# One attention and mixture-of-experts block: each raw chunk of `w13` fetched in two halves, behind the rounding of the probabilities

## What is computed

```python
mod = (_silu(L0_c) @ L0_wmod).reshape(8, 6, 1, -1)
sa, ca, ga, sb, cb, gb = (mod[:, i] for i in range(6))      # ga, gb kept away from zero
h = _layernorm(x) * (1 + ca) + sa
x = x + ga * infini_attention(h, W_q, W_k, W_v, W_o, beta)  # 16 heads, segments of 64 tokens
h = _layernorm(x) * (1 + cb) + sb
x = x + gb * moe(h, router_w, w13, w2)                      # 8 experts, the best 2 of each token
# infini_attention, per segment, with a memory M and z carried along:
#   A = beta * (s(q) M) / (s(q) z) + (1 - beta) * softmax(causal q k^T) v
#   M += s(k)^T (v - (s(k) M) / (s(k) z));  z += sum s(k)
# moe: logits = h router_w^T; gate, up = split(h w13[e]); y = (silu(gate) * up) w2[e]
```

## Time and profile before

| | us |
|---|---|
| median of 3 executions | 1365.4 |
| the three executions | 1365.4, 1361.44, 1370.28 |
| the profiled execution's own time | 1369.37 |
| its span in the profile | 1367.3 |

### The profile page before, as it was taken

How to read it: one execution, slowest core, us unless ns; L and a number is a source line. 1 busy time by engine, 2 the same in 40 slices (tenths; PEclk the granted TensorE clock), 3 DMA queues, 4 the chain that set the end, 5 groups by cost and what they waited for, 6 DMA issues and landing times. The chain is left out here.

```text
span 1367.3 us, 54718 instructions
## 1 busy us (share of the span) xinstructions
PE 1192.2 (87%) x20142; PEld 1016.3 (74%) x20142; DVE 939.0 (69%) x2509; ACT 706.6 (52%) x1391; POOL 927.2 (68%) x989
## 2 busy tenths in 40 slices
PE   3499999999889998989613899999999999999995
PEld 0277778787767777767413699999999999999994
DVE  2389889998888998878668655555555555555552
ACT  2267878887878887877632222323322232322321
POOL 3158989998988898888910466666666666666643
PEclk8599999999999999999855999999999999999998
DMA  9811333334443434443461454545455455555540
GB/s 225 175 55 51 76 91 94 91 96 109 110 97 88 104 104 99 109 99 97 112 216 16 105 99 91 98 92 98 91 101 101 92 95 95 98 94 98 99 75 1
DMA packets 124476, 134.54 MB, mean 98 GB/s; under 512 B 26090, under 2 KB 103986, under 8 KB 124098
## 3 DMA queue, kind: packets, MB, share of 16 engines
q0 software_dynamic: 32592, 56.77, 22.0%
q1 hardware_dynamic: 89762, 67.46, 20.1%
q10 hardware_dynamic: 1872, 6.82, 1.8%
HBM read 63.60 MB, written 44.04 MB: 79 GB/s over the span
## 5 line engine op out<-in xcount | busy, mean ns | idle before, releaser
L1131 PE MATMUL psum<-xT,xall 128*128 128x256 f16 x3408 | 396.6, 273 | 2.5 <-DVE xT L1118 0.9
L1131 PEld LDWEIGHTS psum<-xT,xall 128*128 x3408 | 331.1, 98 | 40.9 <-issue 3.2
L1191 POOL DMA_INDIRECT out<-yo,sidx x142 | 226.4, 1594 | 198.4 <-DVE yo L1182 172.1
L1139 ACT ACTIVATE sg<-psum 128x512 f32<-128x512 f32 x142 | 84.7, 597 | 317.6 <-PE psum L1131 282.8
L1144 DVE SCALAR_TENSOR_TENSOR hf<-psum,sg 128x512 f32<-128x512 f32 x142 | 98.2, 691 | 209.2 <-ACT sg L1139 205.3
L1101 POOL DMA_INDIRECT grow<-moe_rows,gidx x142 | 142.6, 1004 | 99.5 <-DVE sidx L992 56.5
L1165 PE MATMUL psum<-w2s,hT 128*128 x1704 | 197.7, 273 | 2.6 <-DVE w2s L1217 2.4
L1165 PEld LDWEIGHTS psum<-w2s,hT 128*128 128x128 f16 x1704 | 166.5, 98 | 22.5 <-issue 3.2
L1151 ACT ACTIVATE hT<-hf 128x512 f16<-128x512 f32 x142 | 89.5, 630 | 111.4 <-DVE hf L1144 104.6
L569 POOL TENSOR_TENSOR pT<-sc,pT 128x1024 f16<-128x1024 f32 x64 | 136.5, 2133 | 10.1 <-ACT pT L565 10.1
L1155 DVE TENSOR_TENSOR hT<-hf,hT 128x512 f16<-128x512 f32 x142 | 98.3, 692 | 57.0 <-ACT hT L1151 40.4
(11 more groups left out here) (217 smaller groups left out, 2429.9 us busy)
## 6 DMA issues: line engine op xcount, KB each, us to landing
stk<-qk SPq DMA_DIRECT2D x384, 64.0 KB
moe_rows<-hrows SPq DMA_DIRECT2D x128, 128.0 KB, 2.4
out<-xall SPq DMA_DIRECT2D x128, 64.0 KB, 2.1
xall<-in_x SPq DMA_DIRECT2D x8, 896.0 KB, 18.1
raw<-in_w ACTq DMA_DIRECT2D x13, 512.0 KB, 5.5
raw<-in_w SPq DMA_DIRECT2D x8, 512.0 KB, 7.9
grow<-moe_rows,gidx POOLq DMA_INDIRECT x142
out<-yo,sidx POOLq DMA_INDIRECT x142
```

Source lines behind the costliest of these rows:

```text
L1131: i = k.e.matmul(bank[:, n * LONG:(n + 1) * LONG], w13s[:, bass.ds(ex_reg * (G * 4 * I) + ((2 * c + b_) * 2 * I + col), P)], xT[:, k.b, a, ...
L1139: done(k.e.activation(sg[:, half, :], bGate[half][:, :], ACT.Silu, scale=1.0 / W_SCALE), "sg")
L1191: k.e.indirect_dma_start(out_rows, bass.IndirectOffsetOnAxis(ap=sidx[:, n:n + 1], axis=0), yo[:, k.v, q, :], None, bounds_check=B * T - 1, ...
```

## The change

A chunk is now fetched by two DMAs of 128x512 (256 KB) instead of one of 128x1024. The first half (columns 0 to 511, the gate's) is asked for in round 33 + 3n and the second (the up half) in round 34 + 3n, both directly behind `p_high` rather than at the end of a round. The waits of `raw_load` stand before the first half alone. `raw_high` keeps its round, 38 + 3n, and moves from the round's end to directly behind `logit_copy`; it waits for both halves. `raw_low` stays where it was, at the end of VectorE's round.

```diff
-ROUND_LOAD, ROUND_HI, ROUND_LO = 34, 38, 41
+ROUND_LOAD, ROUND_HI, ROUND_LO = 33, 38, 41
...
+    def chunk_of(first, i):
+
+        n, part = divmod(i - first, EVERY)
+        return (n, part) if 0 <= n < NEARLY else (None, part)
     def raw_load(e, i):
-        for j in range(4):
-            e.wait_ge(s_out[j], 32 * (i + 1))
-        if i >= NRAW:
-            e.wait_ge(s_rlo, i - NRAW + 1)
-        e.dma_start(raw[:, i % NRAW, :], w13_chunk(w13, i)).then_inc(s_raw[i % NRAW], 16)
+        n, half = chunk_of(ROUND_LOAD, i)
+        if n is None or half > 1:
+            return
+        if half == 0:
+            for j in range(4):
+                e.wait_ge(s_out[j], 32 * (n + 1))
+            if n >= NRAW:
+                e.wait_ge(s_rlo, n - NRAW + 1)
+        cols = slice(half * I, (half + 1) * I)
+        e.dma_start(raw[:, n % NRAW, cols], w13_chunk(w13, n)[:, cols]).then_inc(s_raw[n % NRAW], 16)
     def raw_high(e, i):
-        e.wait_ge(s_raw[i % NRAW], 16 * (i // NRAW + 1))
-        w13_high(e, w13s, raw[:, i % NRAW, :], i).then_inc(s_rhi, 1)
+        n, part = chunk_of(ROUND_HI, i)
+        if n is not None and part == 0:
+            e.wait_ge(s_raw[n % NRAW], 32 * (n // NRAW + 1))
+            w13_high(e, w13s, raw[:, n % NRAW, :], n).then_inc(s_rhi, 1)
...
-    chunk_work = {"scalar": ((ROUND_LOAD, raw_load), (ROUND_HI, raw_high)), "vector": ((ROUND_LO, raw_low),)}
+    chunk_work = {p_high: raw_load, logit_copy: raw_high, var_eps2: raw_low}
...
             for lag, stage in stages:
                 if 0 <= i - lag < NT:
                     stage(Tile(e, i - lag, full))
-            for first, work in works:
-                if (i - first) % EVERY == 0 and 0 <= i - first < EVERY * NEARLY:
-                    work(e, (i - first) // EVERY)
+                if stage in chunk_work:
+                    chunk_work[stage](e, i)
```

More of the change, by code:

```diff
@@ L789, in attention @@
     }
+    def chunk_of(first, i):
+        n, part = divmod(i - first, EVERY)
+        return (n, part) if 0 <= n < NEARLY else (None, part)
     def raw_load(e, i):
-        for j in range(4):
-            e.wait_ge(s_out[j], 32 * (i + 1))
-        if i >= NRAW:
-            e.wait_ge(s_rlo, i - NRAW + 1)
-        e.dma_start(raw[:, i % NRAW, :], w13_chunk(w13, i)).then_inc(s_raw[i % NRAW], 16)
+        n, half = chunk_of(ROUND_LOAD, i)
[8 more added lines that the diff above has]
+        e.dma_start(raw[:, n % NRAW, cols], w13_chunk(w13, n)[:, cols]).then_inc(s_raw[n % NRAW], 16)
     def raw_high(e, i):
-        e.wait_ge(s_raw[i % NRAW], 16 * (i // NRAW + 1))
-        w13_high(e, w13s, raw[:, i % NRAW, :], i).then_inc(s_rhi, 1)
+        n, part = chunk_of(ROUND_HI, i)
+        if n is not None and part == 0:
+            e.wait_ge(s_raw[n % NRAW], 32 * (n // NRAW + 1))
+            w13_high(e, w13s, raw[:, n % NRAW, :], n).then_inc(s_rhi, 1)
     def raw_low(e, i):
-        e.wait_ge(s_rhi, i + 1)
-        w13_low(e, w13s, raw[:, i % NRAW, :], i).then_inc(s_rlo, 1)
-    chunk_work = {"scalar": ((ROUND_LOAD, raw_load), (ROUND_HI, raw_high)), "vector": ((ROUND_LO, raw_low),)}
+        n, part = chunk_of(ROUND_LO, i)
+        if n is not None and part == 0:
+            e.wait_ge(s_rhi, n + 1)
+            w13_low(e, w13s, raw[:, n % NRAW, :], n).then_inc(s_rlo, 1)
+    chunk_work = {p_high: raw_load, logit_copy: raw_high, var_eps2: raw_low}
     def engine_program(name, e):
@@ L805, in engine_program @@
         deepest = max(lag for lag, _ in stages)
-        works = chunk_work.get(name, ())
-        rounds = max([NT + deepest] + [first + EVERY * (NEARLY - 1) + 1 for first, _ in works])
+        rounds = max(NT + deepest, {"vector": ROUND_LO, "scalar": ROUND_HI}.get(name, 0) + EVERY * (NEARLY - 1) + 1)
         for i in range(rounds):
```

## The result

| | before | changed |
|---|---|---|
| median, us | 1363.4 (4 runs) | 1339.7 (4 runs: 1336.0 to 1349.3) |
| ratio, 95% interval | 1 | 0.9842 (0.9804 to 0.9879) |
| span of the profiled execution | 1367.3 | 1334.1 |

The change makes the kernel 1.6% faster, by 23.8 us. A second measurement of the same kernel later gave 1346.7 us and 0.9888 (0.9854 to 0.9922), 15.9 us. The forecast was a gain of 18.8 us and 1348 us (1337 to 1366). The profiled execution of before, at 1369.4 us, is slower than the median and that of the changed kernel, at 1336.0, is the fastest of its four. So differences between the two traces (33.2 us in the span) are larger than the gain in the medians.

A forecast was written before the change was run, and what follows sets the result against it. TensorE was taken as the bound, stopped by waits for the stack's DMAs. -23.7 + 3.1 + 0 + 1.8 = -18.8 us gave 1350.6 from the profiled execution or 1346.6 from the median; 1348 us was taken, range 1337 to 1366.

The forecast's parts named there:

- The cost of the fetches: TensorE in the 35 rounds with fetches: 16.1 us of waits plus 7.6 of clock, 23.7 us, all removed.
- The quiet stalls stay: TensorE in the 35 rounds: 7.3 us of waits and 6.3 of clock have another cause than fetches and remain.
- The halves' own cost: Half fetches share DMA engines with the store and may delay low parts: 0.13 us x 24 = 3.1 us.
- The earlier place: Fetch issued behind p_high, 3.9 us earlier in the round, lands before the stack's low parts; removes the full 23.7 us.
- The issues: ScalarE's 26 DMA issues instead of 13 lie beside p_high and cost zero; without that cover 8.7 us.
- The high part: Behind the logits it starts sk_act 0.35 us late, delaying mem_den and VectorE: 1.8 us worse, bounds -3.8 to +4.2.
- a sign of being wrong: The prediction fails if L517's waits go and VectorE's L596 or update on TensorE takes them over.
- The halved gain: Halves fall in with the store and low parts come late in some rounds: 0.5 us a half, 1357 us; chance 0.20.
- Not the fetches: Stalls may follow from the long round itself, so the change only moves bytes: 1365 us; chance 0.12.
- The slower one: Every half stalls TensorE like a whole fetch, 1.97 us each: +23.6 us, 1389 us; chance 0.08.

The follow-up runs named there:

- e4: Kernel before, but only chunks 0 to 2 are fetched, whole at the round's end; 1347.5 us against 1359.6.
- a2: The changed kernel measured once more, nothing altered; 1346.7 us, ratio 0.9888 to the kernel before.
- e2: Changed kernel with each half fetched at the end of its own round and the high part at the round's end; 1341.4 us against 1359.6 before.
- e6: Changed kernel with both halves fetched one behind the other at one round's end, high part at the round's end; 1361.9 us against 1366.2 before.
- e1: Changed kernel with the chunk fetched whole, directly behind p_high, and the high part at the round's end; 1345.0 us against 1359.6 before.
- e3: Changed kernel with the fetch whole and at the round's end, so only the high part moves; 1361.8 us, ratio 1.0020 to the kernel before.
- e5: Changed kernel with the high part back at the round's end; ratio 0.9863 to the kernel before, median 1346.0 us.
- e11: Whole fetch behind p_high, high part at the round's end, plus a copy of each chunk to HBM scratch; 1365.4 us against 1362.6 before.
- e9: Changed kernel with the chunk fetched whole behind the logits and the high part at the round's end; 1351.6 us against 1362.6 before.

## Why the prediction was right, and where it was not

**The cost of the fetches (23.7 us): right in cause, in size as far as can be told.** In the two traces L517's waits fell by 19.8 us (16.1 were forecast) and the clock's loss by 11.9 (7.6 were forecast): 27.2 us at half speed lose 13.6 us, 3.4 lose 1.7. The rounded shares give nearly the same for before (0.04 of 346.3 is 13.9). TensorE's busy time agrees: the same 7804 matmuls take 296.3 us instead of 307.5. So 31.7 us went from these terms where 20.6 were forecast net of the halves' own cost. e4 shows the cause directly. Per fetch, it gives 2.2 us in the traces (20.0 in nine) and 1.3 in the medians (12.1 in nine); the 1.97 of the prediction lies between.

**"The quiet stalls stay" (7.3 + 6.3 us): too careful.** In the 35 rounds 3.6 us of waits and 1.7 of clock are left for quiet rounds and halves together, and e4 has 0.3 us of waits in 26 rounds without a fetch. In the 24 rounds that no edit touches, the waits were 5.0 us before, 2.1 in the changed kernel and 4.1 in a2: the rate that I extrapolated is itself a matter of chance in one trace.

**The halves' own cost (3.1 us): not measured apart.** The 3.6 us that are left bound it from above, as far as waits go.

**The earlier place as the reason: half of the truth.** The prediction gave the gain to the place and treated halving as something to be paid for. e2 shows that halves at the old place stall little as well, e6 that in time this isn't due to their shorter rows (in its profile the question stays open), e1 that a whole chunk at the new place doesn't stall the stack. Two conditions make the stall, many bytes at once and low parts of the stack asked for together with them or behind them, and each edit lifts one of the two. That the sum came out in spite of this is in part luck: it counted one sufficient reason and charged the other as a cost. The stops inside a batch, which a whole chunk makes at the early place and halves don't, the prediction did not see at all.

**The issues (0): right.** They lie beside `p_high`.

**The high part (1.8 us): mis-sized.** `mem_den` follows the logits' start by 1.49 us in a round with a high part (474.27 to 475.76) and by 1.35 in one without, 0.14 us late instead of 0.35. But the waits for VectorE grew by 7.3 us (12.3 + 7.5 + 0.8 against 9.5 + 3.8). The prediction named this as a sign of being wrong, and in this part it was: a third of what L517 no longer waits for went to `update` and L596. It goes with a longer low part, 1480 ns in the median instead of 1408 and up to 2628. The two meetings with GpSimd's power are some of it (L549 waits 1.43 and 1.67 us there); what makes up the rest stays open. Neither e3 nor e5 resolves it in time.

**Sum.** 19.8 + 11.9 of gain, less 7.3 at VectorE: 24.4 of the 24.9 us by which the 35 rounds are shorter in this pair of traces. In the medians the gain is less. Against the forecast of 18.8 the two measurements stand at 23.8 and 15.9; that it lies between them rests on a gain and a loss that were both larger than forecast.

**The rivals.** The halved gain didn't come. "Not the fetches" is refuted by e4. The slower one, each half at the price of a whole, is refuted by e2 even at the old place. The Trainium skill's fixed time per DMA (DMA: Bandwidth & Descriptors, Anatomy of one DMA), from which the prediction took an argument against splitting, is fitted there to DMAs that GpSimd issues, and these are ScalarE's. The direction is right for the transfer all the same, but it does not reach the kernel: at the early place a whole chunk lands in 4.1 us (e1) and two halves in 3.1 each, 6.2 together, and the kernel is no slower. The Trainium skill's remark that DMAs of all issuing engines run on the same 16 DMA engines and interleave (same page, Issuing engines are not separate DMA queues) agrees with e11, where ScalarE's q10 and SyncE's q1 both move packets in the same 8.3 us.

## What to carry to other kernels

Here a background transfer cost what it held up, not what it took: look which small transfer is due next, and either move the background one out of its way or cut it so that little of it is ever in flight; one of the two was enough here. Read the wait in its consumer's row, and count the clock's loss behind long waits with it (11.9 us of 31.7 here). When work that no one waits for is moved on a full engine, look what the pieces behind it now meet.

## What was unexpected of the hardware

- TensorE stopped for 2.35 us inside a batch of 48 matmuls, while 1 MB of data passed and the instruction queue delivered nothing for 8.3 us (e11). With a single 512 KB fetch it stopped inside a batch for up to 0.9 us (e1) and 2.0 us (e9).
- VectorE's 128x1024 `scalar_tensor_tensor` took 2.33 us instead of 1.25 beside GpSimd's 128x1 power, which took 1.55 instead of 0.54. In other meetings the power was as long and VectorE's 1.47 us.
- ScalarE's queue issued a DMA 0.01 us behind the start of the ACTIVATE ahead of it in the program, and took 0.33 us for it at no cost to the engine.
